# A Mamba block's convolution split between ScalarE and GpSimd, with the chunk's other pieces moved

## The reference, cut to what matters

```python
xz = x @ in_proj_w.T                      # 2048 x 1024
u, z = jnp.split(xz, 2, axis=-1)          # 512 channels each
u = jax.nn.silu(causal_dwconv(u, conv_w, conv_b))    # 4 taps along the time
x_dbl = u @ x_proj_w.T                    # dt (16), B (16), C (16)
delta = jax.nn.softplus(dt @ dt_proj_w.T + dt_proj_b)
# for each time: h = exp(delta*A) * h + (delta*u) * B;   y = sum over 16 states of h * C
y = y + u * D
y = y * jax.nn.silu(z)
return y @ out_proj_w.T
```

## Time and profile before

| what | value |
|---|---|
| median of 3 runs | 1681.53 us (1681.5 to 1683.56) |
| the profiled execution: its time, its span | 1688.74 us, 1687.0 us |
| granted TensorE clock over the span | 0.892 of full speed |
| busy: PE, ACT, DVE, POOL | 1370.0, 914.2, 815.6, 424.0 us |
| first scan starts, last product by C ends | 49.88 us, 697.65 us |
| DVE busy from 209 to 373 us, in 164 us | 153.88 us |
| PE busy from 373 to 549 us, in 176 us | 132.92 us |

### The profile page before, as it was taken

One profiled execution on the slowest core, in us unless ns is written; L12 is line 12 of the kernel. 1 busy time (PEld: TensorE's weight loads), 2 busy tenths in 40 slices (PEclk: granted clock), 3 DMA queues, 4 the chain that ended last, 5 costly groups with the idle time before them and its releaser, 6 DMA issues.

```text
span 1687.0 us, 15369 instructions
## 1 busy us (share of the span) xinstructions
PE 1370.0 (81%) x5571; PEld 646.2 (38%) x5571; DVE 815.6 (48%) x845; ACT 914.2 (54%) x1268; POOL 424.0 (25%) x290
## 2 busy tenths in 40 slices
PE   6566665789578966989633999999999987989999
PEld 2122222334223532555421222223223233558887
DVE  3899989996999799512722001001001015561001
ACT  4525542684258434402322999898998963760310
POOL 0645753674456556210530000000000001000000
PEclk9679887899879987969765999999999987989999
DMA  5323331332133323020599000000000000010801
GB/s 192 102 75 114 129 108 65 112 129 84 62 115 112 99 100 125 38 51 25 65 103 99 1 1 1 1 1 0 0 0 0 0 0 1 1 50 2 347 13 38
DMA packets 35631, 107.95 MB, mean 64 GB/s; under 512 B 3650, under 2 KB 14146, under 8 KB 32915
## 3 DMA queue, kind: packets, MB, share of 16 engines
q1 hardware_dynamic: 35572, 107.19, 22.9%
HBM read 93.60 MB, written 2.36 MB: 57 GB/s over the span
## 4 chain that ended last, share of the span: by engine, by line
PE 46%; DVE 24%; ACT 15%; issue 8%; DMA 5%; SPq 2%; POOL 0%; DVEq 0%; ACTq 0%; POOLq 0%
DVE ps L904 11%; PE ps L1591 9%; PE ps L1576 9%; ACT arena L739 6%; PE ps L1395 4%; PE ps L1700 3%; DVE arena L915 3%; DMA arena<-arena 3%; PE ps L1741 3%; PE ps L1350 3%; DVE arena L849 2%; ACT ps L595 2%; PE ps L1718 2%; PE ps L1281 2%; PE ps L1729 2%
## 5 line engine op out<-in xcount | busy, mean ns | idle before, releaser
L739 ACT ACTIVATE arena<-ps,bound 128x1024 f32<-128x1024 f32 (+1 forms) x416 | 421.0, 1215 | 25.9 <-PE ps L1576 25.9
L439 POOL TENSOR_TENSOR arena<-arena 128x1024 f32<-128x1024 f32 x128 | 327.1, 2556 | 236.7 <-DVE ps L904 190.0
L1350 PE MATMUL ps<-arena,ident 128*128 128x512 f32 x512 | 261.0, 651 | 67.1 <-DVE arena L915 67.0
L904 DVE TENSOR_TENSOR_SCAN ps<-ps,arena 128x1024 f32<-128x1024 f32 x128 | 300.7, 2350 | 25.7 <-ACT ps L595 15.5
L1576 PE MATMUL ps<-arena 97*128 (+3 forms) x832 | 218.3, 384 | 22.2 <-issue 20.1
L1591 PE MATMUL ps<-arena 128*32 128x512 f32 (+1 forms) x1664 | 222.5, 607 | 1.1 <-ACT arena L739 0.9
L595 ACT ACTIVATE ps<-arena 128x512 f32<-128x512 f32 x256 | 166.3, 682 | 71.1 <-DVE arena L915 67.2
L426 POOL TENSOR_TENSOR rstd<-ve,mhalf 128x4 f32<-128x4 f32 (+3 forms) x18 | 23.4, 1302 | 674.4 <-DVE ve L1199 468.4
L1174 DVE COPY arena<-ps 128x512 f32<-128x512 f32 x16 | 11.1, 692 | 354.3 <-PE ps L1591 354.3
L1350 PEld LDWEIGHTS ps<-arena,ident 128*128 128x128 f32 x512 | 100.5, 205 | 213.2 <-issue 113.2
L915 DVE TENSOR_TENSOR arena<-ps,arena 128x1024 f32<-128x1024 f32 x128 | 156.0, 1219 | 7.0 <-DVE ps L904 0.5
(11 more groups left out here) (182 smaller groups left out, 1505.9 us busy)
## 6 DMA issues: line engine op xcount, KB each, us to landing
arena<-bc_scratch SPq DMA_DIRECT2D x128, 512.0 KB, 3.7
arena<-in_mw SPq DMA_DIRECT2D x16, 1024.0 KB, 8.8
arena<-arena SPq DMA_DIRECT2D x48, 128.0 KB, 15.1
arena<-arena SPq DMA_DIRECT2D x12, 400.2 KB, 16.8
arena<-in_w SPq DMA_DIRECT2D x2, 1024.0 KB
out<-xt SPq DMA_DIRECT2D x4, 512.0 KB, 2.9
xt<-in_x SPq DMA_DIRECT2D x1, 1536.0 KB
arena<-in_ctx SPq DMA_DIRECT2D x1, 1200.8 KB, 7.7
```

The lines of the kernel that those rows point to most:

```text
L439: pool.tensor_tensor(dbu[:, w % DR], du[:, DP * p:DP * p + DP], over(bg[:, w // BG % 2, n % BG], DP), ALU.mult).then_inc(S["dbu_ready"], 1)
L739: act.activation(flat(prob[0:n, v % 2, 2 * h:2 * h + 2]), ps[0:n, 2 * (r % 3):2 * (r % 3) + 2, :].rearrange("p a b -> p (a b)"), ACT.Exp, ...
L904: dve.tensor_tensor_scan(decay_banks(w), decay_banks(w), flat(dbu[:, w % DR]), carry[:, DP * p, n:n + 1], ALU.mult, ALU.add).then_inc(S["s ...
L1350: last = mm(bank(x), ident[:, :], state(2 * j + s)[:, x], start=False, stop=(j % HP == HP - 1 and (j in SUMMED or s == 1)))
```

## The change

The first tap, with the bias, becomes a scaled copy on ACT straight out of PSUM; ACT also scales the three other taps into six tiles of a block pair (`conv_taps`, steps 9, 11, 13 and 16), in buffers that the step size uses at other times. POOL adds them up, one tap in each of the steps 10 to 21. Chunk 0 has its three taps on DVE still. POOL's product of step w waits for the product by C of step w - 3 and no longer for the scan of step w - 3. The other pieces move: rank_b_c from step 17 to 22 (PE) and 18 to 23 (ACT), the hidden products from 23, 25, 27, 29 to 19, 26, 28, 30 (PE), their Gelus from 24, 26, 28, 30 to 20, 27, 29, 31.

```diff
-                    if i == 10 and c + 1 < NC:
+                    if i == 12 and c + 1 < NC:
                         store_bc(c + 1)
...
-                    pool.wait_ge(S["scan_done"], w - DR + 1)
+                    pool.wait_ge(S["hc_ready"], w - DR + 1)
...
+            def convolution(c, d, j):                      # POOL
+                out = channels_of(c, d // DP)[:, d % DP]
+                if j:
+                    pool.wait_ge(S["conv_step"], (TAPS - 1) * (c * DB + d) + j)
+                pool.wait_ge(S["tap_ready"], (TAPS - 1) * ((c - 1) * DB + d) + j + 1)
+                pool.tensor_tensor(out, out, tap_tiles[d % 2][j], ALU.add).then_inc(S["conv_step"], 1)
...
+                    if 10 <= i < 10 + DB * (TAPS - 1) and c + 1 < NC:
+                        convolution(c + 1, (i - 10) // (TAPS - 1), (i - 10) % (TAPS - 1))
...
+                act.activation(u, work(d), ACT.Identity, bias=ch("conv_b")[:, d:d + 1],
+                               scale=ch("conv_w", TAPS)[:, d, TAPS - 1:TAPS])
...
+            def conv_taps(c, d):
...
+                for j in range(TAPS - 1):
+                    act.activation(tap_tiles[d % 2][j], upad[:, d, j:j + C], ACT.Copy,
+                                   scale=ch("conv_w", TAPS)[:, d, j:j + 1]).then_inc(S["tap_ready"], 1)
...
+                    if i in (9, 11, 13, 16) and more:
+                        conv_taps(c + 1, (9, 11, 13, 16).index(i))
+                    if i in (16, 22) and more:
+                        for d in range(0, DP) if i == 16 else range(DP, DB):
                             channel(c + 1, d)
-                    if i == 18 and more:
+                    if i == 18 and c:
+                        turned_h1(c - 1)
+                    if i == 20 and c:
+                        hidden(c - 1, 0)
+                    if i == 23 and more:
                         rank_b_c(c + 1)
...
+                    if i in (27, 29, 31) and c:
+                        hidden(c - 1, i - 25)
...
-                if i in (9, 10, 11, 12) and more:
-                    convolution(c + 1, i - 9)
```

More of the change, by code:

```diff
@@ L834, in normed_input, with convolution @@
                                       ALU.subtract, ALU.mult).then_inc(S["a0_ready"], 1)
[L836 to L850, removed]
+            def convolution(d):
+                out = channels_of(0, d // DP)[:, d % DP]
+                dve.wait_ge(S["u_raw"], d + 1)
+                for j in reversed(range(TAPS - 1)):
+                    if j < TAPS - 2:
+                        dve.wait_ge(S["conv_step"], (TAPS - 1) * d + TAPS - 2 - j)
+                    dve.scalar_tensor_tensor(out, upad[:, d, j:j + C], conv_w[:, d, j:j + 1],
+                                             out, ALU.mult, ALU.add).then_inc(S["conv_step"], 1)
             def conv_keep(c):
-                dve.wait_ge(S["conv_step"], (c + 1) * TAPS * DB)
+                dve.wait_ge(S["conv_step"], (c + 1) * (TAPS - 1) * DB)
                 dve.tensor_copy(upad[:, :, 0:TAPS - 1], upad[:, :, C:C + TAPS - 1]).then_inc(S["hist_in"], 1)
@@ L992, in between @@
                     step_heads(c, 1)
-                if i in (9, 10, 11, 12) and more:
-                    convolution(c + 1, i - 9)
-                if i == 13 and more:
+                if i == 22 and more:
                     conv_keep(c + 1)
@@ L1008, in between @@
                         normed_input(c + 2)
-                if i == 17 and c:
+                if i == 16 and c:
                     first_norm(c - 1)
@@ L1031, in _ @@
             for d in range(DB):
-                convolution(0, d)
+                convolution(d)
             conv_keep(0)
@@ L1380, in hidden @@
                     pe.wait_ge(S["h1t_ready"], c * DK + DK)
-                    if c + 2 < NC:
-                        pe.wait_ge(S["sp_in"], (c + 2) * DB + DP)
+                if f == 2 and c + 2 < NC:
+                    pe.wait_ge(S["sp_in"], (c + 2) * DB + DP)
                 if f >= 2:
@@ L1434, in _ @@
                         gates(c + 1, i - 12)
-                    if i == 17 and more:
+                    if i == 17 and c:
+                        turn_h1(c - 1)
+                    if i == 19 and c:
+                        hidden(c - 1, 0)
+                        hidden(c - 1, 1)
+                    if i == 22 and more:
                         rank_b_c(c + 1)
-                    if i == 19 and c:
-                        turn_h1(c - 1)
-                    if i == 21 and more:
+                    if i == 24 and more:
                         step_input(c + 1, 0)
-                    if i in (23, 25, 27, 29) and c:
+                    if i in (26, 28, 30) and c:
+                        hidden(c - 1, i - 24)
                         hidden(c - 1, i - 23)
-                        hidden(c - 1, i - 22)
                     if i in (30, 31) and c:
```

44 lines of the change are left out of this document (24 added, 20 removed).

## The result

The changed kernel takes 1653.45 us (1652.95 to 1658.98, 4 runs), the kernel before beside it 1681.51 (1679.31 to 1683.56, 4 runs): 0.984 of the time, 95% interval 0.9817 to 0.9865. Forecast were 1645 us and a range of 1622 to 1664. The profiled execution took 1653.42 us with a span of 1651.6, at its median; that of before lay 7 us above its own. So profile to profile the change is 35.4 us (36 were worked out), by medians 28.

What follows compares the result with a forecast made beforehand. DVE was taken to bound the loop. Gains of 55 + 16 = 71 us less losses of 35 gave net 36; from the 1681.5 us median that made 1645 us, range 1622 to 1664.

Steps and rivals of the forecast that it cites:

- Gain 55 for the taps: Convolution taps leave DVE in the loop: 12 blocks of 4.55 us, 54.6 us, counted as 55 gained.
- 16 for the later start: POOL's product starts later, so DVE work outside steps 10 to 21 runs faster: 16 us gained, ends 0 and 25.
- POOL's adds, 2 us: POOL's adds in steps 10 to 21, about 1.27 us each, cost 2 us for all chunks; ends 0 and 36.
- rival B: Smaller gain: POOL or PE becomes the bound in the middle of a chunk, 18 us more, 1663 us; chance 0.17.
- The loads, 10.5 us: Step 24's product by C waits for its rows, loaded behind SP's wait for the rank copy: 3 x 3.5 us lost.
- The last Gelus, 7.2 us: Last Gelus in step 31 delay DVE's second residual: 2 x 3.6 us lost, and about 1.3 behind the last scan.
- hidden(0), hidden(1) ahead of scan 22, 10.6 us: These products in PE's step 19 make scan 22 later in three chunks: 10.6 us lost.
- out_project, 3.6 us: out_project waits for the last u_raw in ACT's step 10; second residual input 1.8 us late in chunks 1 and 2.
- I cost it at nothing: ACT's 4 scaled copies and 12 taps per chunk: no cost; without cover, up to 0.5 us in 8 steps per chunk.
- A (the late pieces are absorbed): Bigger gain: half of the 35 us loss gone, 5 more from released operations, 1623 us; chance 0.17.
- D: Nothing measurable: gain and late pieces cancel, all losses doubled, 1681 us; chance 0.02.
- C (slower, POOL and DVE in each other's way): In steps 10 to 21 adds behave like 3.2 us, exposing 58 us: 1703 us; chance 0.04.

Runs made afterwards that it cites:

- e4: The kernel before with one change: POOL's product waits for the product by C, not the scan, of three steps before; taps stay on DVE; 1640.63 us.
- e7: The changed kernel with the convolution's taps back on DVE in steps 9 to 12, moved pieces and later POOL start kept; 1668.16 us.
- e3: The changed kernel with POOL's product waiting again for the scan of three steps before, all else as changed; 1674.22 us.
- e8: The changed kernel with one more POOL operation of the add's size ahead of each of the 36 adds; 1673.64 us.
- e1: The changed kernel with store_bc moved from step 12 to 13, after load_b(13) and load_c(12); 1644.13 us.
- e2: The changed kernel with hidden(0) and hidden(1) in PE's step 18, ahead of the skip product, instead of step 19; 1638.32 us.
- e9: e6 with the convolution's taps back on DVE in steps 9 to 12; 1627.23 us.
- e6: e5_both with hidden(2), hidden(3) moved to PE's step 20, the other four to 26 and 28, Gelus in steps 20, 21, 27, 29; 1606.8 us.
- e5_both: The changed kernel with the corrections of e1 and e2 together; 1625.04 us.

## Why the prediction was right, point by point

**The sum** held: a loop 33.6 us shorter against a forecast net of 36, a gain on DVE of 68.5 us against 71, and 35 more of idle time against 35 of loss. The forecast then took 36 us, read in an execution 7 us above its median, off the median. The changed kernel's execution was at its own median, and that is most of the 8 us between 1645 and 1653.45. What the 7 us were is not shown.

**Gain 55 for the taps, 16 for the later start.** Their sum was right, but what it says of either edit holds in one order only. The 4.55 us of a block from the earlier trace rows were measured while POOL's product ran against them; 1.9 of them the later start alone takes away (e4). In busy time of DVE, the start taken first is worth 45 us and the taps 25 behind it (e7 against the changed kernel). With the early start kept, the change of the taps and pieces is worth 43 (596.87 - 553.66, e3), and the start behind it 25. The forecast took the taps first, and there the terms were 43 against 55 and 25 against 16. The grouped lines of e3 against those of before say where the 12 us went. The waiting moved to others: L889 takes 6.2 us more in all (14.6 against 8.4), and L864, L963 and L857, in the steps where POOL now adds, 5.4 more than their counterparts. The later start took L889's 6 us back, and 6.0 in L864 where 3.1 were forecast. So 71 against 68.5 is in part luck: two terms off by 12 and 9 us in opposite directions.

**POOL's adds, 2 us.** An add takes 1347 ns on average (1.27 us were forecast for a free one; the adds of e8 that follow another one take 1269) and no scan waits for POOL beyond the start. e8 shows the margin: some 40 us more of adds bring 20 us to light. The 18 us of rival B would have wanted about as much more work on POOL.

**The loads, 10.5 us.** 10.5 in three waits in the trace; mending them gave 9.3 (e1).

**The last Gelus, 7.2 us.** The second residuals in the loop wait 26.2 us against 19.2: 7.0. The 1.3 us behind the loop are not to be seen: the first second residual there waits 11.56 us against 11.65.

**hidden(0), hidden(1) ahead of scan 22, 10.6 us.** The three scans wait 5.99 + 5.54 + 5.89 = 17.4 us against 0 + 2.88 + 2.52 = 5.4 before: 12.0. ACT's rows of chunk 1 show the chain: the Gelu's table is there, and the first Gelu waits for PE's hidden.

```profile
289.27 1.28 ACT L637 ACT_TABLE_LOAD   x1
296.83 0.69 ACT L637 ACTIVATE arena<-ps,chan 128x512 f32<-128x512 f32 x1 [6.27 <-PE ps L1409]
298.54 0.69 ACT L637 ACTIVATE arena<-ps,chan 128x512 f32<-128x512 f32 x1 [1.03 <-PE ps L1409]
299.13 0.17 ACT L608 ACTIVATE arena<-ps 128x2 f32<-128x2 f32 x1
299.31 1.28 ACT L621 ACT_TABLE_LOAD   x1
300.61 1.30 ACT L621 ACTIVATE ps<-arena 128x512 f32<-128x512 f32 x2
```

From the start of the load at 299.31 to the next ACTIVATE at 300.61 are 1.30 us. The Trainium skill ("ScalarE: Activation LUTs", What ACT_TABLE_LOAD costs) adds a drain of about 1.38 us; this row, like the earlier trace rows, leaves no place for it, and the measurement decides.

**out_project, 3.6 us.** 5.6 in two waits of 2.80 us. PE ends one pair of tiles at 250.15 and the next at 257.04, 6.9 us later; DVE needs 4.1 us from the first residual to where it could start the second.

**What the terms missed**: scan 18 of chunk 0 waits 2.06 us for ACT, whose step 16 now carries two table loads, gates, taps and channels; it works without a gap from 119.73 us until that scan's decays are done at 128.97. So "I cost it at nothing" was 2 us short. Scan 16 of chunk 2 waits 1.23 us where it waited 0.56; ACT had idled 3.42 us for the late residual of step 13 just before. Other, small waits of scans for ACT became shorter, and in all these waits grew by 31.7 - 20.3 = 11.4 us.

**The rivals.** A (the late pieces are absorbed) is refuted by e1 and e2: the stalls gave back 9.3 us of 10.5 and 15.1 of 17.4. B fails in both its forms: no scan waits for POOL in steps 12 to 21 or for PE anywhere, and the later start gave more than forecast. D is outside the interval. C (slower, POOL and DVE in each other's way) named the largest effect in this kernel, but the adds did not bring it: they take 1347 ns and not 2.6 us. The conflict was there before; the new wait ended it. The Trainium skill's warning that work moved between GpSimd and DVE might not help, since they share a read port ("Perfetto Trace Analysis", Optimizing Scalar/DVE Operations), is borne out in that the two hinder each other (e4; that it is a port no run shows). The outcome here is another: e9 against e6 shows 20 us for the offload.

## What to carry to other kernels

When an operation's duration in a trace depends on what a neighbour engine does, cost the edit that ends the conflict by itself before any that moves work: here one changed wait was worth 42 us alone, and the whole change, that wait included, 28. Two edits that relieve the same resource don't have a worth each; price them in both orders, or run both alone. And pieces moved for an offload have to be mended one by one afterwards: the new order cost some 28 us, and three small moves gave back 47 (1606.8 us).

## What the runs showed of the hardware

Tiles lie in SBUF (arena in the rows) or in PSUM (ps). In these traces a POOL operation, all of whose tiles are in SBUF, and certain DVE operations exclude each other for a whole instruction. Between the kernel before and e4, which differ by one wait, the mean durations on DVE are: tap with two SBUF tensors (L849) 1133 against 752 ns, scaled copy of 128 x 512 (L845) 1398 against 552, sum of two SBUF tensors (L877, mean of 8) 2195 against 1266. Operations with an operand in PSUM keep theirs: the scan 2350 and 2348 ns, the product by C 1219 and 1218. The delay falls on whichever comes second: POOL's product took 2556 ns on average before and 2350 in e4.

This says which instruction pays while the product starts at the end of a scan. The first operation of DVE behind the scan goes ahead of it, the second waits for it. In step 8 of the kernel before L870 takes 1.21 us and L877 behind it 3.17 to 3.18; where L877 is alone behind its scan, in step 27, it takes 1.21. In the convolution's steps 11 and 12 the first tap takes 0.52 us and the three others together 4.3 instead of 2.33; in step 9, where L885 goes ahead, it is the first tap that takes 2.55. L889 of e3 is the same case. Two pieces of other work put into one step can thus cost more than in two steps.

The Trainium skill ("SBUF — State Buffer", Who interferes with whom) says of the pair of ports that these two engines share: whoever issues first gets it for the whole instruction, and the other fully blocks. The trace agrees in the timing, with L961 of e8 as its plainest row; the ports themselves are in no row.

The kernel before scattered more than the others: 1673.7 to 1687.8 us over 17 runs, against 1669.3 to 1676.4 for e8 in 12 and 1624.7 to 1627.6 for e5_both in 5. That the conflicts are the cause was not tested.
